# Attention steps in fours: four rounds of scores and maxima, then four value rounds, with twice the buffers between

## The chip, the cores and the metric

One core of a Trainium2 chip runs the whole kernel. The metric is the device time of one launch in microseconds (us). The kernel before ran three times; the profile is one more execution, taken by the hardware profiler.

## The reference

The layer runs over four batches of 2048 tokens with 512 channels. Each batch goes through attention with 16 heads of 32 channels, and then through a mixture of experts (128 experts of which 48 are kept, 8 for each token).

```python
mod = (silu(c) @ wmod).reshape(4, 6, 1, -1)
h = layernorm(x) * (1 + ca) + sa
q, k, v = to_heads(h @ Wqkv.T + bqkv)
att = softmax(where(causal, rope(q) @ rope(k).T * HD ** -0.5, -inf))
x = x + ga * ((att @ v) @ Wo.T + bo)
h = layernorm(x) * (1 + cb) + sb
x = x + gb * mixture_of_experts(h)
```

## The kernel before, in words

**Stages.** A batch passes through three stages: projections of q, k and v with the rotation of q and k (the steps of `front()`, L120); attention, head by head (`stream()`, L160); then the mixture of experts with routing. The change lies in the second.

**Attention.** Scores of a head are computed with keys on the partitions: a *score tile* is 128 keys by the 512 queries of one of four query chunks, 40 tiles of a head (the masked ones narrower). Each is one matmul on PE (L1334; masked tiles have a second, L1337, that adds the mask) into one of three PSUM banks S2, from which ScalarE (ACT) writes the exponential into a probability buffer `Pt` (L1141). The softmax needs each query's maximum beforehand; it comes from 40 *maxima tiles* of the same head with queries on the partitions (L1311, into three PSUM banks S1), reduced by VectorE (DVE) at L1653 or, for masked and some other tiles, L1649. The maxima of a half of the head are turned into a row (L1316 on PE, then DVE) that is moved by SP as a 97th row into the stacked queries `QK` (`max_row`, L736), so that the score matmul subtracts it. The first half of the row serves query chunks 0 and 1, the second half chunks 2 and 3: the first score of chunk 2, which is the first of round 5, waits for it (L1322).

**Rounds.** The score tiles of a chunk go through in *rounds* of two or three tiles (`SHAPES`, L91), 15 rounds of a head: rounds 0 and 1 belong to chunk 0, 2 to 4 to chunk 1, 5 to 8 to chunk 2, and 9 to 14 to chunk 3. For a round GpSimd (POOL) sums its probability tiles into a buffer `Sm` (`plus`, L1006), and then PE runs the *value round*: two or three value matmuls side by side in strips of 32 columns (L1358) and the sum of the probabilities in the fourth strip (L1361, L1362). A value round waits for its sum (L1343). An exponential waits until the value round that last read its `Pt` buffer is done (L1140), a sum until the one that last read its `Sm` buffer is done (L999).

**Order.** `stream()` writes out one list of steps for all engines by hand; each engine runs its own kinds of step in the order of that list. An iteration of its loop (L203) takes two rounds n and n+1: their score tiles alternate with what stands in `beside` for them, then come their sums, then the two value rounds n-2 and n-1, then what stands in `closing`. In `beside` are the maxima of the *next* head, spread from round 2 of a head to round 0 of the following one (`TILES_FROM`, L155), and the steps that make the row. In `closing` are the copies of a finished chunk's output out of PSUM to `od` (ACT, L1128), `LAG` = 3 rounds after the chunk's last round, then the joins, reciprocals and scalings of groups of four heads, and at the end of a batch the first output projections.

**SP's queue.** The loads of heads are issued by SP, in order (L788 to L819). In its loop for head hh SP waits until all scores of head hh-2 have been issued (they read the same half of `QK`), issues the 12 loads of head hh (`stack`, L698), the second half of the row of head hh-1 (L736), the moves of `od` for chunk 3 of head hh-2 and chunk 0 of head hh-1 (`move`, L731, three or four DMAs each, behind the copy), chunk 1, the first half of head hh's row, and the move of chunk 2 of head hh-1. Then come, for one head in four, a load of the next group's values (L719) and, for one in four, a store of a group (L751). Only then does the loop for head hh+1 begin.

**Buffers.** There are 12 `Pt` and 4 `Sm` buffers of 512 columns in float32 (L94), `Pt[:, t % NPT]` and `Sm[:, round % NSM]`.

Of the kernel before, what the change touches and what calls it, by code (L numbers as in the profile page):

```python
# [7 lines left out]
F32 = mybir.dt.float32  # L8
# [4 lines left out]
ACT = mybir.ActivationFunctionType  # L13
AX = mybir.AxisListType

P = 128
NB, T, C, H, HD = 4, 2048, 512, 16, 32
KT = C // P
CH = 512
NCH = T // CH  # L20
# [27 lines left out]
ONE = 1  # L48
# [42 lines left out]
SHAPES = ((2, 2), (3, 2, 3), (3, 3, 3, 3), (3, 3, 3, 3, 2, 2))  # L91
ROUNDS = [(j, tuple(range(sum(shape[:r]), sum(shape[:r + 1])))) for j, shape in enumerate(SHAPES) for r in range(len(shape))]
NR = len(ROUNDS)
NPT, NSM, LAG = 12, 4, 3  # L94
N_JOIN = 2 * NCH - 1
NS1 = NS2 = 3
NCK = NCH * NG
# [9 lines left out]
def tile_at(j, k):  # L107

    return 2 * j * (j + 1) + k
# [50 lines left out]
def stream():  # L160

    closing = [[] for _ in range(NR * H + 12)]
    beside = [[] for _ in range(NR * H)]
    negated = {}
    for i in range(LAST_CHUNK, NTILE):
        beside[(i - LAST_CHUNK) // 4].append(("max", 0, i))
    beside[2].append(("most", 0, 1))
    beside[3] += [("row", 0, 1), ("negated", 0, 1)]
    for hh in range(1, H):
        late = TILES_FROM if hh > 1 else FIRST_TILES_FROM  # L170
        at, span = NR * (hh - 1) + late, NR + 1 - late
        for i in range(NTILE):
            beside[at + i * span // NTILE].append(("max", hh, i))
            if i in (FIRST_HALF - 1, NTILE - 1):
                half, n = int(i >= FIRST_HALF), at + i * span // NTILE
                beside[n + 1].append(("most", hh, half))
                beside[n + 2].insert(0, ("row", hh, half))
                negated[n + 2] = ("negated", hh, half)
    for n, step in negated.items():
        beside[n].insert(2, step)  # L180
    for hh in range(H):
        for j in range(NCH):
            n = NR * hh + LAST_ROUND[j] + LAG
            closing[n].append(("copy", hh, j))
            if hh == H - 1 and j < NCH - 1:
                closing[n + 2] += [("join", NG - 1, j), *(("inverse", NG - 1, j, i) for i in range(TPC))]
                closing[n + 3].append(("scale", NG - 1, j))
            elif hh % GH == GH - 1 and hh < H - 1:
                closing[n + 3].append(("join", hh // GH, j))
                for i in range(TPC):  # L190
                    closing[n + 3 + i // 2].append(("inverse", hh // GH, j, i))
                closing[n + 5].append(("scale", hh // GH, j))
    last = NR * (H - 1)
    for i, t in enumerate(OUT_AT):
        closing[last + t].append(("out", *divmod(i, TPC)))
        if i == TPC - 1:
            closing[last + t].append(("moments",))
    closing[last + NR].append(("normed",))
    closing[NR * (H - 3)].append(("fold",))
    closing[last - 1].append(("widen", 0))  # L200
    closing[last + 5].append(("widen", 1))
    out = []
    for n in range(0, NR * H + 12, 2):  # L203
        if n < NR * H:
            here = [divmod(n, NR), divmod(n + 1, NR)]
            tiles = [("score", hh, r, k) for hh, r in here for k in ROUNDS[r][1]]
            aside = beside[n] + beside[n + 1]
            for i in range(max(len(tiles), len(aside))):
                out += tiles[i:i + 1] + aside[i:i + 1]
            out += [("plus", *of) for of in here]  # L210
        if 2 <= n < NR * H + 2:
            out += [("value", *divmod(n - 2, NR)), ("value", *divmod(n - 1, NR))]
        out += closing[n] + closing[n + 1]
    return out


# [84 lines left out]
def adaln_block(nc, x, wqkv, bqk, bv, wo, bo, cT, wmod, gwT, o2n_col, o2n_row, wgu, wdn, cos, sin, kst, out):  # L301
    with ExitStack() as ctx:
# [74 lines left out]
        stA = place("stA", [P, TPC, 6], F32)  # L377
        mvA = place("mvA", [P, TPC, 2], F32)
        rsA = place("rsA", [P, TPC], F32)
        xin = [place("xin0", [P, TPC, C], F32), xin1]  # L380
        SPARE_AT = at[0]
        vst = [vst0, place("vst1", [P, TPC, NG * P], F32)]


        at[0] = W_AT
        Pt = place("Pt", [P, NPT, CH], F32)
        Sm = place("Sm", [P, NSM, CH], F32)
        o1 = place("o1", [P, T], F32)
        o2 = place("o2", [P, T], F32)
        assert at[0] <= W_END  # L390


        at[0] = OD_AT
# [64 lines left out]
        at[0] = SPARE_AT  # L458
        B1 = place("B1", [P, TPC, 6, P], BF16)
        B2 = place("B2", [P, TPC, 6, 2, P], BF16)  # L460
        stC = place("stC", [P, TPC, 6], F32)
        mvC = place("mvC", [P, TPC, 2], F32)
        rsC = place("rsC", [P, TPC], F32)
# [429 lines left out]
        def _(pool):  # L893
# [21 lines left out]
            for b in batches(pool):  # L915
# [37 lines left out]
                for step in STEPS:  # L953
# [13 lines left out]
                    elif kind == "mul":  # L967

                        _, n, i = step
                        j = n // NG  # L970
                        chunk = NCK * b + n
                        table_of = cs[:, j % 2, i:i + 1].broadcast_to([P, 2, CH])
                        if n % NG == 0 and i == 0:
                            pool.wait_ge(cs_in[j % 2], ONE + 32 * (NCH // 2 * b + j // 2 + 1))
                        if i == 0:

                            pool.wait_ge(f_act, ONE + N_QT * b + taken_by(("proj", n, 1)))
                            if n >= 2:
                                pool.wait_ge(q_lo, ONE + chunk - 1)
                            nc.gpsimd.tensor_tensor(t1[:, n % 2], qraw[:, n % 2], table_of, ALU.mult).then_inc(rope_mul, 1)  # L980
                        else:
                            pool.wait_ge(q_shuf, ONE + chunk + 1)
                            nc.gpsimd.tensor_tensor(qs[:, :, :], qs[:, :, :], table_of, ALU.mult).then_inc(rope_mul, 1)
                    elif kind == "fold":

                        pool.wait_ge(rows_in, ONE + 64 * (b + 1))
                        nc.gpsimd.tensor_tensor(rows[:, 1], rows[:, 0], rows[:, 1], ALU.mult).then_inc(gabo, 1)
                        for k in range(KT):
                            nc.gpsimd.tensor_tensor(wot[:, k], wot[:, k], rows[:, 0], ALU.mult).then_inc(wo_gated, 1)
                    elif kind == "widen":  # L990
                        widen(step[1])
                    elif kind == "plus":

                        _, hh, r = step
                        j, ks = ROUNDS[r]
                        at = NR * hh + r
                        pool.wait_ge(exp_done, ONE + NPT_B * b + NTILE * hh + tile_at(j, ks[-1]) + 1)
                        if at >= NSM:
                            pool.wait_ge(pv_done, ONE + NV * b + at - NSM + 1)  # L999
                        of = [Pt[:, (NTILE * hh + tile_at(j, k)) % NPT] for k in ks]  # L1000
                        for i in range(1, len(ks)):
                            first, _ = extent(j, ks[i])
                            total = Sm[:, at % NSM, first:CH]
                            if i == 2:
                                pool.wait_ge(sum_done, ONE + N_SUM * H * b + N_SUM * hh + SUMS[r] - 1)
                            nc.gpsimd.tensor_tensor(total, of[0][:, first:CH] if i == 1 else total, of[i][:, first:CH], ALU.add).then_inc(sum_done, 1)  # L1006
                    elif kind == "join":
                        join(*step[1:])
                    elif kind == "scale":
                        scale(*step[1:])  # L1010
                    elif kind == "moments":
                        spread_of(0)
# [45 lines left out]
        def _(act):  # L1058
# [18 lines left out]
            for b in batches(act):  # L1077
# [11 lines left out]
                for step in STEPS:  # L1089
# [39 lines left out]
                    elif kind == "score":  # L1129
# [4 lines left out]
                        if t == 0:  # L1134

                            act.wait_ge(w_out, ONE + 16)
                        act.wait_ge(s2_ready, ONE + NPT_B * b + t + 1)
                        if t >= NPT:

                            act.wait_ge(pv_done, ONE + NV * b + NR * ((t - NPT) // NTILE) + ROUND_OF[(t - NPT) % NTILE] + 1)  # L1140
                        nc.scalar.activation(Pt[:, t % NPT, first:CH], S2[t % NS2][:, first:CH], ACT.Exp, scale=SCALE).then_inc(exp_done, 1)  # L1141
                    elif kind == "normed":
                        norm(0)
                meet(act, 2 * b + 2)
# [69 lines left out]
        def _(pe):  # L1214
# [25 lines left out]
            for b in batches(pe):  # L1240
# [18 lines left out]
                for step in STEPS:  # L1259
# [79 lines left out]
                    elif kind == "value":  # L1339
# [12 lines left out]

                            pe.wait_ge(o_free, ONE + NCH * H * b + nn - 1)
                        begins = r == FIRST_ROUND[j]
                        of = [Pt[:, (NTILE * hh + tile_at(j, k)) % NPT] for k in ks]
                        firsts = [extent(j, k)[0] for k in ks]
                        for i, k in enumerate(ks):
                            mm(O[j % 2][i * HD:(i + 1) * HD, firsts[i]:CH], V[:, g % 2, k, h * HD:(h + 1) * HD], of[i][:, firsts[i]:CH],  # L1358
                               start=begins, stop=r == LAST_USE[j, i])
                        if firsts[1] > firsts[0]:  # L1360
                            mm(O[j % 2][3 * HD:P, firsts[0]:firsts[1]], onesv[:, :], of[0][:, firsts[0]:firsts[1]], start=begins, stop=False)  # L1361
                        mm(O[j % 2][3 * HD:P, firsts[1]:CH], onesv[:, :], Sm[:, at % NSM, firsts[1]:CH], start=begins, stop=r == LAST_ROUND[j]).then_inc(pv_done, 1)  # L1362
                    elif kind == "out":
                        rows_out(*step[1:])
                meet(pe, 2 * b + 2)
# [521 lines left out]
```

## Time and profile before

| | |
|---|---|
| three runs | 4260.27, 4262.83, 4269.38 us (median 4262.83) |
| the profiled execution, its span | 4268.8 us |
| PE busy | 3857.2 us, 90% |
| VectorE busy | 2754.6 us, 65% |
| GpSimd busy | 2780.5 us, 65% |
| ScalarE busy | 1806.6 us, 42% |

The span runs from the first to the last instruction of the profiled execution; it is 6 us above the median of the runs and lies between the lowest and the highest. Busy shares are means over all stages. Attention of a batch is some 570 us of it, four times. The wait of an engine is the idle time before an instruction, put down to what released it.

### The profile page before, as it was taken

Reading aid. Unit: us, or ns where it says so; the run is one execution under the profiler, and the core shown is the slowest. Engines: PE = TensorE matmul, PEld = TensorE weight load, DVE = VectorE, ACT = ScalarE, POOL = GpSimd, SP = SyncE. Lnnn points to the kernel's source line nnn. Section 1 sums busy time; section 2 is a strip of 40 time slices with the busy share of each in tenths; the row PEclk is TensorE's granted clock in tenths of the full one; section 3 lists DMA queues with packets and bytes.
Section 4 is the critical chain, followed back from the end, with each engine's and each line's share of the span. In section 5 each row is a group of like instructions: output and inputs, shape, how many; then the busy total and the mean of one; then the engine's idle time right before and its main releaser. Section 6 shows DMA issues by size and latency. Waiting matters only on the chain. (4 is left out here: it accounts for less than half of the span.)

```text
span 4268.8 us, 81098 instructions
## 1 busy us (share of the span) xinstructions
PE 3857.2 (90%) x21344; PEld 2337.8 (55%) x21344; DVE 2754.6 (65%) x5889; ACT 1806.6 (42%) x3526; POOL 2780.5 (65%) x2251
## 2 busy tenths in 40 slices
PE   5989999987999999879899999879899999859998
PEld 2754544456744454457554544457545444547776
DVE  3767677466757767476667776567676774645655
ACT  1345555423355555332355555233455555211111
POOL 3768788824668878716678888427687888215554
PEclk8989999998999999989899999889899999979999
DMA  6543333242533333334433333425333332349997
GB/s 210 180 119 91 91 99 108 79 181 98 178 93 100 86 102 96 120 135 148 139 91 100 99 98 108 155 82 179 115 90 91 99 105 81 102 135 258 258 257 190
DMA packets 305135, 549.12 MB, mean 129 GB/s; under 512 B 59572, under 2 KB 99636, under 8 KB 301492
## 3 DMA queue, kind: packets, MB, share of 16 engines
q1 hardware_dynamic: 283192, 485.62, 37.8%
q0 software_dynamic: 21504, 58.40, 5.8%
q8 instruction: 183, 3.00, 0.3%
q14 instruction: 256, 2.10, 0.2%
HBM read 311.86 MB, written 174.85 MB: 114 GB/s over the span
## 5 line engine op out<-in xcount | busy, mean ns | idle before, releaser
L1141 ACT ACTIVATE Pt<-PS 128x512 f32<-128x512 f32 (+3 forms) x2560 | 1205.9, 542 | 1004.6 <-PE PS L1334 554.9
L1006 POOL TENSOR_TENSOR Sm<-Pt 128x512 f32<-128x512 f32 (+3 forms) x960 | 1029.5, 1078 | 389.6 <-ACT Pt L1141 383.6
L1653 DVE TENSOR_REDUCE part<-PS 128x1 f32<-128x512 f32 x1536 | 1003.5, 685 | 334.6 <-PE PS L1311 329.6
L1311 PE MATMUL PS<-QK 96*128 96x512 f32 (+3 forms) x2560 | 1026.8, 419 | 88.6 <-DVE mT L1668 24.4
L1334 PE MATMUL PS<-QK 97*128 97x512 f32 (+3 forms) x2560 | 991.8, 409 | 38.7 <-DMA QK<-mT 18.5
L1358 PE MATMUL PS<-Pt,V 128*32 128x512 f32 (+3 forms) x5120 | 870.0, 554 | 42.5 <-POOL Sm L1006 42.3
L1362 PE MATMUL PS<-Sm,onesv 128*32 128x512 f32 (+3 forms) x1920 | 818.8, 535 | 0.0
L1649 DVE CUSTOM_DVE_ANT_0 PS<-PS,consts 128x128 f32<-128x128 f32 (+3 forms) x1024 | 503.8, 495 | 415.8 <-PE PS L1311 408.5
L1334 PEld LDWEIGHTS PS<-QK 97*128 97x128 f32 x2560 | 488.0, 193 | 474.7 <-issue 345.7
L1006 POOL TENSOR_TENSOR Sm<-Sm,Pt 128x512 f32<-128x512 f32 (+1 forms) x640 | 713.2, 1114 | 50.2
L1311 PEld LDWEIGHTS PS<-QK 96*128 96x128 f32 x2560 | 496.0, 195 | 299.5 <-DVE part L1653 110.8
L1358 PEld LDWEIGHTS PS<-Pt,V 128*32 128x32 f32 x5120 | 217.1, 111 | 366.0 <-issue 238.1
L1295 PE MATMUL PS<-hTu,W 128*128 128x512 f32 x1024 | 328.3, 402 | 25.3 <-DVEq L644 13.4
L980 POOL TENSOR_TENSOR t<-qraw,cs 128x1024 f32<-128x1024 f32 x64 | 184.4, 2882 | 171.7 <-ACT qraw L1106 162.6
L1042 POOL DMA_INDIRECT out<-z,it x96 | 139.1, 1448 | 208.0 <-DVE z L1831 113.3
L1601 DVE RECIPROCAL den<-den 128x128 f32<-128x128 f32 x256 | 221.2, 914 | 69.4 <-DMA den<-od 67.9
L1461 PEld LDWEIGHTS PS<-XT,Wg 128*96 128x96 f32 x1536 | 250.7, 164 | 26.7 <-issue 26.3
L1461 PE MATMUL PS<-XT,Wg 128*96 128x192 f32 x1536 | 259.2, 327 | 1.3 <-ACT XT L1192 0.7
L1337 PE MATMUL PS<-mtbf,idbf 128*128 128x128 bf16 (+1 forms) x1024 | 239.1, 236 | 0.0
L1295 PEld LDWEIGHTS PS<-hTu,W 128*128 128x128 f32 x1024 | 194.7, 193 | 73.3 <-issue 17.6
L1128 ACT ACTIVATE od<-PS 128x512 f32<-128x512 f32 x256 | 155.6, 608 | 138.3 <-PE PS L1362 138.3
L1106 ACT ACTIVATE qraw<-PS,bqg 128x512 f32<-128x512 f32 x128 | 86.9, 679 | 279.7 <-PE PS L1295 248.9
(169 smaller groups left out, 4962.6 us busy)
## 6 DMA issues: line engine op xcount, KB each, us to landing
QK<-qkd SPq DMA_DIRECT2D x720, 128.0 KB, 3.1
qkd<-st SPq DMA_DIRECT2D x64, 1024.0 KB, 4.5
Wg<-wgu SPq DMA_DIRECT2D x48, 768.0 KB
o<-od SPq DMA_DIRECT2D x448, 64.0 KB, 2.0
W<-wd SPq DMA_DIRECT2D x3, 6144.0 KB, 21.5
Wd<-wdn SPq DMA_DIRECT2D x48, 384.0 KB
xin<-x SPq DMA_DIRECT2D x16, 1024.0 KB, 7.9
vd<-vst SPq DMA_DIRECT2D x16, 1024.0 KB, 6.1
```

The source lines that it names most:

```text
L1006: nc.gpsimd.tensor_tensor(total, of[0][:, first:CH] if i == 1 else total, of[i][:, first:CH], ALU.add).then_inc(sum_done, 1)
L1141: nc.scalar.activation(Pt[:, t % NPT, first:CH], S2[t % NS2][:, first:CH], ACT.Exp, scale=SCALE).then_inc(exp_done, 1)
L1295: last = mm(bank, W[:, w, k, i, g * P:(g + 1) * P], (hTu, hTl)[h][:, j % 2, k], start=(k, w, h) == (0, *TERMS[0]), stop=(k, w, h) == (KT - ...
L1311: mm(s1[:, 0:w], QK[0:3 * HD, hh % 2, 0, qb * P:(qb + 1) * P], QK[0:3 * HD, hh % 2, 1, c * CH:c * CH + w], start=True, stop=True).then_inc ...
L1334: last = mm(S2[t % NS2][:, first:CH], QK[0:3 * HD + 1, hh % 2, 1, k * P:(k + 1) * P], QK[0:3 * HD + 1, hh % 2, 0, j * CH + first:(j + 1) * ...
L1337: last = mm(S2[t % NS2][:, first:first + masked], idbf[:, :], mtbf[:, 2 * P - masked:2 * P], start=False, stop=True)
L1358: mm(O[j % 2][i * HD:(i + 1) * HD, firsts[i]:CH], V[:, g % 2, k, h * HD:(h + 1) * HD], of[i][:, firsts[i]:CH], start=begins, stop=r == LAS ...
L1362: mm(O[j % 2][3 * HD:P, firsts[1]:CH], onesv[:, :], Sm[:, at % NSM, firsts[1]:CH], start=begins, stop=r == LAST_ROUND[j]).then_inc(pv_done, 1)
L1461: last = mm(banks[i][:, q, :], Wg[:, u % HELD, k, o:o + HALF], XT[:, u % 2, k // 2, k % 2, :], start=k == 0, stop=k == KT - 1)
L1601: v.reciprocal(den[:, cols], den[:, cols]).then_inc(den_inv, 1)
L1649: v.tensor_tensor_reduce(out=s1[:, 0:w], in0=s1[:, 0:w], in1=K[:, K_NEG + CH - w:K_NEG + CH], scale=1.0, scalar=-3e38, op0=ALU.add, op1=AL ...
L1653: v.reduce_max(part[:, qb, cc:cc + 1], s1[:, 0:w], AX.X).then_inc(s1_dve, 1)
```

## The change

`BURST` = 4 takes the place of the 2 that stood in the loop of `stream()`: an iteration takes four rounds, whose score tiles alternate with the `beside` of all four, then the four sums, then the four value rounds before these, then the `closing` of four rounds. There are 24 `Pt` and 8 `Sm` buffers, and `LAG` is 4. The second halves of both sets are placed over memory of the projection stage (an input buffer and a buffer of values for `Pt`, the rotation's tables for `Sm`); since that stage's values are stored to HBM from there, ACT waits once a batch for that store before the first exponential into the second half.

```diff
-NPT, NSM, LAG = 12, 4, 3
+BURST = 4
+NPT, NSM, LAG = 24, 8, 4
...
-    for n in range(0, NR * H + 12, 2):
+    for n in range(0, NR * H + 12, BURST):
         if n < NR * H:
-            here = [divmod(n, NR), divmod(n + 1, NR)]
+            here = [divmod(n + i, NR) for i in range(BURST)]
             tiles = [("score", hh, r, k) for hh, r in here for k in ROUNDS[r][1]]
-            aside = beside[n] + beside[n + 1]
+            aside = sum(beside[n:n + BURST], [])
             for i in range(max(len(tiles), len(aside))):
                 out += tiles[i:i + 1] + aside[i:i + 1]
             out += [("plus", *of) for of in here]
-        if 2 <= n < NR * H + 2:
-            out += [("value", *divmod(n - 2, NR)), ("value", *divmod(n - 1, NR))]
-        out += closing[n] + closing[n + 1]
+        if BURST <= n < NR * H + BURST:
+            out += [("value", *divmod(n - BURST + i, NR)) for i in range(BURST)]
+        out += sum(closing[n:n + BURST], [])
     return out
...
-        Pt = place("Pt", [P, NPT, CH], F32)
-        Sm = place("Sm", [P, NSM, CH], F32)
+        Pt0 = place("Pt0", [P, NPT // 2, CH], F32)
+        Sm0 = place("Sm0", [P, NSM // 2, CH], F32)
...
+        at[0] = C_END
+        Sm1 = place("Sm1", [P, NSM // 2, CH], F32)
+        assert at[0] <= W_AT
+        at[0] = XIN_AT
+        Pt1 = place("Pt1", [P, NPT // 2, CH], F32)
+        PT_END = at[0]
+        Pt = [half[:, i] for half in (Pt0, Pt1) for i in range(NPT // 2)]
+        Sm = [half[:, i] for half in (Sm0, Sm1) for i in range(NSM // 2)]
...
                         if t == 0:
 
                             act.wait_ge(w_out, ONE + 16)
+                        if t == NPT // 2:
+
+                            act.wait_ge(v_out[1], ONE + 32 * (NCH // 2) * (b + 1))
```

In the changed kernel's lines the scores are L1350 and L1353, the maxima L1327, the value rounds L1374 to L1378.

PE's list in the kernel before, from value round 8 of head 4 on (32x384, 32x256, 32x128 and the two sums are that round; `V` are the values, `onesv` ones):

```order
L1343 REGISTER_ALU
L1358 MATMUL PS<-Pt,V 32x384
L1358 MATMUL PS<-Pt,V 32x256
L1358 MATMUL PS<-Pt,V 32x128
L1361 MATMUL PS<-Pt,onesv 32x128
L1362 MATMUL PS<-Sm,onesv 32x256
L1343 REGISTER_ALU
L1353 REGISTER_ALU
L1358 MATMUL PS<-Pt,V 32x512 x3
L1362 MATMUL PS<-Sm,onesv 32x512
L1333 REGISTER_ALU
L1334 MATMUL PS<-QK 128x512
```

One value round stands behind it, and then a stretch of scores begins (rounds 12 and 13 of head 4), followed by two value rounds, a second stretch and two more value rounds, before the scores of rounds 1 and 2 of head 5.

PE's list in the changed kernel, from the same value round on:

```order
L1374 MATMUL PS<-Pt_91,V 32x384
L1374 MATMUL PS<-Pt_91,V 32x256
L1374 MATMUL PS<-Pt_91,V 32x128
L1377 MATMUL PS<-Pt_91,onesv 32x128
L1378 MATMUL PS<-Sm_90,onesv 32x256
L1359 REGISTER_ALU
L1369 REGISTER_ALU
L1374 MATMUL PS<-Pt_91,V 32x512 x3
L1378 MATMUL PS<-Sm_90,onesv 32x512
L1359 REGISTER_ALU
L1374 MATMUL PS<-Pt_91,V 32x512 x3
L1378 MATMUL PS<-Sm_90,onesv 32x512
```

The scores of rounds 12 to 14 of head 4 and round 0 of head 5 now stand ahead of this round; three value rounds stand behind it.

PE's list in the changed kernel, behind the last of these value rounds, from the second score tile of round 1 of head 5 to the first maximum of head 6 (`mtbf,idbf` is the mask, `consts,mx` the row of maxima, the ISA row a wait for the head's loads):

```order
L1353 MATMUL PS<-mtbf,idbf 128x128
L1349 REGISTER_ALU
L1350 MATMUL PS<-QK 128x128
L1353 MATMUL PS<-mtbf,idbf 128x128
L1283 REGISTER_ALU
L1331 REGISTER_ALU
L1332 MATMUL PS<-consts,mx 8x128
L1349 REGISTER_ALU
L1350 MATMUL PS<-QK 128x512
L1283 REGISTER_ALU
L1326 ISA
L1327 MATMUL PS<-QK 128x128
```

The same rows stand in the same order ahead of that maximum in the kernel before; there two stretches of scores and four value rounds lie between it and value rounds 8 and 9 of head 4. SP's list has the same order in both kernels.

## Rows read from the trace of the kernel before

**Rows 1.** The page: the span, busy time of the engines, TensorE's granted clock in 40 slices.

```profile
span 4268.8 us, 81098 instructions
...
PE 3857.2 (90%) x21344; PEld 2337.8 (55%) x21344; DVE 2754.6 (65%) x5889; ACT 1806.6 (42%) x3526; POOL 2780.5 (65%) x2251
...
PEclk8989999998999999989899999889899999979999
```

**Rows 2.** Waits of PE: engine, line, releaser, total us, times, longest us.

```profile
PE PS L1358 <- POOL Sm L1006: 42.3, 26, 4.5
...
PE PS L1334 <- DMA QK<-mT: 18.5, 4, 5.2
...
PE PS L1311 <- DMA QK<-qkd: 14.1, 21, 1.5
...
PEld PS L1311 <- DVE part L1653: 110.8, 379, 1.1
```

**Rows 3.** Timeline of PE and ACT, 428 to 442: start, duration, instruction, [idle before <-releaser].

```profile
428.18 0.51 PE L1358 MATMUL PS<-Pt,V 128*32 128x384 f32 x3
...
429.20 0.60 ACT L1128 ACTIVATE od<-PS 128x512 f32<-128x512 f32 x1 [0.66 <-PE PS L1362]
...
435.26 0.22 PE L1334 MATMUL PS<-QK 97*128 97x128 f32 x1
...
441.43 0.33 PE L1311 MATMUL PS<-QK 96*128 96x128 f32 x1 [1.32 <-DMA QK<-qkd]
```

**Rows 4.** Timeline of SP's issues, 432 to 445.

```profile
432.68 0.66 SPq L719 DMA_DIRECT2D V<-vd  x1
435.79 7.88 SPq L698 DMA_DIRECT2D QK<-qkd  x12
443.86 0.73 SPq L736 DMA_DIRECT2D QK<-mT  x1
```

**Rows 5.** Timeline of PE around two value rounds, 612 to 615.

```profile
612.00 0.40 PE L1334 MATMUL PS<-QK 97*128 97x512 f32 x1
612.23 0.28 PE L1311 MATMUL PS<-QK 96*128 96x256 f32 x1
612.45 0.63 PE L1358 MATMUL PS<-Pt,V 128*32 128x512 f32 x3
...
613.76 0.61 PE L1358 MATMUL PS<-Pt,V 128*32 128x512 f32 x3
...
614.30 0.50 PE L1334 MATMUL PS<-QK 97*128 97x512 f32 x1
614.64 0.23 PE L1337 MATMUL PS<-mtbf,idbf 128*128 128x128 bf16 x1
```

**Rows 6.** Timeline of SP and PE at the start of a batch's attention, 250 to 262.

```profile
250.33 7.79 SPq L698 DMA_DIRECT2D QK<-qkd  x12
258.33 0.76 SPq L736 DMA_DIRECT2D QK<-mT  x1
...
254.81 0.44 PE L1311 MATMUL PS<-QK 96*128 96x128 f32 x1 [0.54 <-DMA QK<-qkd]
...
261.14 0.79 PE L1334 MATMUL PS<-QK 97*128 97x512 f32 x1 [4.45 <-DMA QK<-mT]
```

**Rows 7.** Windows: from:to us, busy (x count) PE PEld DVE ACT POOL, PEclk, DMA, GB/s.

```profile
382.70:389.00 6.30, 5.07 (x34) 2.66 (x30) 6.30 (x13) 3.20 (x6) 6.14 (x7) 1.00 0.14 34
...
676.00:683.60 7.60, 6.34 (x34) 3.23 (x30) 7.44 (x14) 3.26 (x6) 6.92 (x8) 0.78 0.13 32
...
441.30:446.00 4.70, 4.48 (x28) 2.50 (x29) 2.40 (x10) 2.84 (x6) 2.53 (x2) 1.00 0.67 194
```

**Rows 8.** Timeline of PE at a batch's tail, 832.

```profile
832.52 0.78 PE L1358 MATMUL PS<-Pt,V 128*32 128x512 f32 x3 [2.72 <-POOL Sm L1006]
```

**Rows 9.** Timeline of DVE, 381 and 611: a group's reciprocals, maxima.

```profile
381.88 3.38 DVE L1601 RECIPROCAL den<-den 128x128 f32<-128x128 f32 x4
...
611.26 1.89 DVE L1653 TENSOR_REDUCE part<-PS 128x1 f32<-128x512 f32 x3
```

More of the change, by code:

```diff
@@ L379, in adaln_block @@
         rsA = place("rsA", [P, TPC], F32)
+        XIN_AT = at[0]
         xin = [place("xin0", [P, TPC, C], F32), xin1]
@@ L460, in adaln_block @@
         B2 = place("B2", [P, TPC, 6, 2, P], BF16)
+        assert at[0] >= PT_END
         stC = place("stC", [P, TPC, 6], F32)
@@ L999, in _ @@
                             pool.wait_ge(pv_done, ONE + NV * b + at - NSM + 1)
-                        of = [Pt[:, (NTILE * hh + tile_at(j, k)) % NPT] for k in ks]
+                        of = [Pt[(NTILE * hh + tile_at(j, k)) % NPT] for k in ks]
                         for i in range(1, len(ks)):
                             first, _ = extent(j, ks[i])
-                            total = Sm[:, at % NSM, first:CH]
+                            total = Sm[at % NSM][:, first:CH]
                             if i == 2:
@@ L1140, in _ @@
                             act.wait_ge(pv_done, ONE + NV * b + NR * ((t - NPT) // NTILE) + ROUND_OF[(t - NPT) % NTILE] + 1)
-                        nc.scalar.activation(Pt[:, t % NPT, first:CH], S2[t % NS2][:, first:CH], ACT.Exp, scale=SCALE).then_inc(exp_done, 1)
+                        nc.scalar.activation(Pt[t % NPT][:, first:CH], S2[t % NS2][:, first:CH], ACT.Exp, scale=SCALE).then_inc(exp_done, 1)
                     elif kind == "normed":
@@ L1354, in _ @@
                         begins = r == FIRST_ROUND[j]
-                        of = [Pt[:, (NTILE * hh + tile_at(j, k)) % NPT] for k in ks]
+                        of = [Pt[(NTILE * hh + tile_at(j, k)) % NPT] for k in ks]
                         firsts = [extent(j, k)[0] for k in ks]
@@ L1361, in _ @@
                             mm(O[j % 2][3 * HD:P, firsts[0]:firsts[1]], onesv[:, :], of[0][:, firsts[0]:firsts[1]], start=begins, stop=False)
-                        mm(O[j % 2][3 * HD:P, firsts[1]:CH], onesv[:, :], Sm[:, at % NSM, firsts[1]:CH], start=begins, stop=r == LAST_ROUND[j]).then_inc(pv_done, 1)
+                        mm(O[j % 2][3 * HD:P, firsts[1]:CH], onesv[:, :], Sm[at % NSM][:, firsts[1]:CH], start=begins, stop=r == LAST_ROUND[j]).then_inc(pv_done, 1)
                     elif kind == "out":
```

## The prediction

> **What bounds the kernel now.** I read the page's head first: TensorE is busy 90% of the span, VectorE and GpSimd 65% each, and the clock line sits at 8 or 9 tenths throughout [rows 1]. So PE's own list of work sets the time, and the next question is what makes PE wait. The waits of PE show that attention hardly waits: maxima on VectorE's emptying no more than 1.1 us at a time, maxima on the head's loads (QK<-qkd) 14.1 us in 21 waits, scores on the row of maxima (QK<-mT) 18.5 us in 4, value rounds on GpSimd's sums 42.3 us in 26 [rows 2]. The last three are small *because* the work that they wait for is started early enough. The change moves where that work starts, so I then followed one head through the timelines.
>
> Call H the head whose scores run. During H come the maxima of head H+1, and for those its q and k have to be loaded. SP's queue is in order (L788 to L819): the copy of chunk 2 of head H-1 goes out (L731, four DMAs), then, every fourth head, V (L719) or a group's store, then the 12 loads of head H+1 (L698), then the second half of H's row of maxima (L736). The move cannot start before ACT has copied the chunk out of PSUM (L1128), and that waits for value round 8 of head H-1. Thus *value round 8 of head H-1 on PE, copy, move, loads, first maximum of head H+1* is one chain, and *... loads, row, score of round 5 of head H* another.
>
> For H = 5: round 8 of head 4 starts at 428.18, the copy runs 429.20 to 429.80, the move follows, V is issued at 432.68 for 0.66 [rows 3, 4]; there SP waits until 435.79, since the loads may not overwrite head 4 before its last score at 435.26 [rows 3, 4]. The 12 loads take 7.88, the row is issued at 443.86, and the first maximum runs at 441.43, 5.6 after the loads began and after a wait of 1.32 [rows 3, 4]. So 11.6 us lay between the copy's end and the first maximum, and PE still came early by 1.3.
>
> **The cost of a late chain.** Prices: round 8's start to the copy's end 1.62, of it some 0.8 after PE is free of the round (a round is 0.93: two from 612.45 to 614.30 [rows 5]); copy's end to SP's next issue behind the move 2.9 (429.80 to 432.68), 3.5 with a group's store (0.6, an estimate from the other issues), 3.8 with V [rows 3, 4]; loads to first maximum 5.6 behind a V load, 4.5 without (250.33 to 254.81 at a batch's start) [rows 4, 6]; loads to the row's issue 7.7 to 8.1; the row's issue to the score that needs it 2.8 (258.33 to 261.14) [rows 6].
>
> In the changed kernel four score rounds stand together, then four value rounds, and the fours run over heads of 15 rounds, so four cases come in turn. A matmul of a score stretch is 0.24 [rows 5].
> H = 1, 5, 9, 13: round 8 is the first of its four (the first piece of PE's list above). Behind it PE has three value rounds (2.7) and four matmuls (1.0), then the first maximum: 3.7 us of work against 0.8 + 3.8 + 5.6 = 10.2. PE waits 6.5.
> H = 4, 8, 12: two value rounds and some 12 matmuls, 1.85 + 2.9 = 4.7, against 0.8 + 3.5 + 4.5 = 8.8: 4.1.
> H = 3, 7, 11: one value round and some 18 matmuls, 0.9 + 4.4 = 5.3, against 0.8 + 2.9 + 4.5 = 8.2: 2.9.
> H = 2, 6, 10, 14: round 8 is the last of its four; a whole score stretch follows and four value rounds, so the first maximum is in time (8.4 against 8.2), but the score of round 5 comes after 4.3 + 3.6 + 3.0 = 10.9, against 0.8 + 2.9 + 7.7 + 2.8 = 14.2: 3.3.
> A batch has 4 x 6.3 (one of the four lacks V) + 3 x 4.1 + 3 x 2.9 + 4 x 3.3 = 59 us, four batches **+237** in 56 waits. In the kernel before the same distances hold one more score stretch, and that covered the chain.
>
> **The clock.** After a wait PE can run at the lower of its two levels: a stretch of the same 34 matmuls takes 6.30 at a granted clock of 1.00 (2.4 GHz) and 7.60 at a mean of 0.78, which is 0.50 (1.2 GHz) in 44% of it [rows 7]: 1.3 us. Not every wait is followed by that: behind the wait of 1.32 at 441.43 the clock is 1.00 for 4.7 us [rows 3, 7]. Bounds: 0, and 56 x 1.3 = 73. The waits here are mostly longer than those, so I take **+45**.
>
> **Ends.** At a batch's start two value rounds now run after, not inside, the 4.45 us wait for the row [rows 6]: 2 x 0.93, +1.8. At the tail the output projection is placed behind more of GpSimd's work, and value rounds already wait 2.72 for their sum there [rows 8]: I take +2.7. Times four: **+18**. Four such places are few; 0 and 36 are the bounds.
>
> **Gains.** A round trip between value and score shapes costs PE 0.30: 0.22 behind a 256-column maximum worth 0.12, the last value row 0.54 where those before it took 0.44 each (612.45 to 613.76, three), the first score 0.34 for 0.24 [rows 5]. 480 round trips become 240: -72 at most. Part comes back: VectorE takes 0.63 for a maximum of 512 columns (1.89 for three), PE issues one every 0.48, and three PSUM banks hold no more than three of them [rows 5, 9]. In the kernel before the two value rounds let VectorE catch up; in fours it falls behind for longer, then catches up for longer. I take **-45** (0 to -72). More buffers loosen the value rounds' wait on sums, 42.3 us in all [rows 2], and the value rounds in fours cover more of the four reciprocals' 3.38, which keep VectorE from the maxima [rows 9]: **-20** (0 to -42). The added wait on ACT for a store of V before the thirteenth exponential comes once a batch and behind SP's own wait for it (L787): nothing, as scores wait for the row of maxima there until 261.14 [rows 6]. The buffers' new places cost nothing: they are the same operations on other addresses, and the inputs that lay there are used up.
>
> **Sum.** 237 + 45 + 18 - 45 - 20 = +235. The profiled execution has a span of 4268.8, 6 above the median of 4262.83 and within the three runs; against the median 4262.8 + 235 = **4498**. What a measurement of this kernel can tell from no change is about 0.2%, 8.5 us. The likeliest case's own range: with each of the 56 chains 1.5 shorter -84, with the clock at 73, no gain from fewer round trips and the ends at 36 +91: 4400 to 4590.
>
> **Rivals.** (A) *Faster: the chain is not late.* The place is SP's loads (L698). If they began earlier than I count, PE would keep only the gains and the ends: 4262.8 - 65 + 18 = 4216 (4190 to 4250). It decides at each head: the time from the copy's end to the first maximum has to be no more than the 3 to 4.5 us of work that PE has left. For it speaks that the 12 loads are not held up by anything else there; against it that their issue alone is 0.65 apiece, one behind the other (7.88 for 12), and that the wait of 1.32 at 441.43 shows no slack today [rows 3, 4]. Chance 0.12.
> (B) *Half the waiting.* The waits fall together with VectorE's arrears: where VectorE sets the stretch anyway, a wait for the loads of 3 to 6 us takes the place of waits for emptying rather than adding to them. Then 118 + 22 + 18 - 45 - 20 = +93: 4356. For it: ten full maxima are 6.3 us of VectorE, the 20 matmuls with them 4.8 of PE [rows 5, 9]. Against: those arrears are at most three banks, 1.9 us [rows 9]. Chance 0.10.
> (C) *The lower clock stays.* After each wait the whole of the next score stretch and its value rounds run low, two stretches of 1.3 more: 56 x 2.6 = 148 in place of 45, 4601. For it: a stretch partly at 0.50 is in the trace [rows 7]; against it: the other stretch of the same work ran at 1.00, so did the one behind the wait at 441.43, and the clock line stands at 8 and 9 tenths [rows 1, 7]. Chance 0.10. The Trainium skill (TensorE: Matmul & The Clock Gate, "HAM oscillation — how this bites in real kernels") says that a kernel whose short runs of matmuls each follow a wait on a DMA starts every one of them at the low clock; by that rule the time would be (C)'s; the trace of before doesn't bear it out at 441.43, where the clock is 1.00 behind the wait, but that wait is short.
> (D) *No change*, gains and waits within 8.5 of each other: 4263, chance 0.02. PE's list shows that the fours are really there, so the change does what it says.
>
> **How the numbers follow.** The likeliest case has 0.66, (A) 0.12, (B) 0.10, (C) 0.10, (D) 0.02. The range 4320 to 4610 holds the likeliest, (B) and (C), 0.86 less their tails. Faster by over 0.2%: 0.12; within: 0.02; slower: 0.86.
>
> **What would show it.** In the waits of PE, maxima on QK<-qkd should grow from 14.1 us to some 150 to 190, and scores on QK<-mT from 18.5 to 60 or 70. SP's loads should begin within 4 us of a copy's end, with no wait for the last score between. The head after a V load should wait longest, near 6.5. Wrong I would be if QK<-qkd stays near 14 us (then A), or if it grows and PE's waits on VectorE fall by as much (B), or if the clock line drops by a tenth in all of attention (C).

## The result, and the profile after

Four runs took 4651.39 to 4658.54 us, median 4654.51; the kernel before, in the same comparison, 4262.15. The ratio is 1.0915, with a 95% interval of 1.090 to 1.093: slower by 392 us. The forecast was slower by 235, 4498, with a range from 4320 to 4610. The direction and the place were right, the size was not.

The page of the changed kernel (the span, the engines, the granted clock in 40 slices), which answers to [rows 1]:

```profile
span 4653.8 us, 81110 instructions
...
PE 3999.0 (86%) x21344; PEld 2506.1 (54%) x21344; DVE 2753.6 (59%) x5889; ACT 1824.4 (39%) x3526; POOL 2784.6 (60%) x2251
...
PEclk8978888888988988888888888889888898879999
```

The span grew by 385. PE has the same 21344 matmuls, but is busy 142 us longer, while VectorE's and GpSimd's busy time stands still (ScalarE's grew by 18); and the clock line has lost about a tenth through most of attention. That is one part. The waits of PE (engine, line, releaser, total us, times, longest), which answer to [rows 2], show another:

```profile
PE PS L1327 <- DMA QK<-qkd: 221.0, 47, 9.0
PE PS L1350 <- DMA QK<-mT: 58.4, 22, 4.8
PE PS L1271 <- issue: 33.1, 3, 11.1
...
PE PS L1271 <- POOL ot L959: 9.4, 1, 9.4
```

Waiting for a head's loads and for the row of maxima came to 279.4 us in place of 32.6, +247; the prediction had +237, without the batches' starts. The value rounds' wait for sums (42.3 before) is gone from the list. The output projections at a batch's end (L1271), which did not appear there, wait 42.5.

The same head as in [rows 3, 4], now from 464 to 478 us. First ACT, then SP's issues, then PE:

```profile
464.77 0.60 ACT L1141 ACTIVATE od<-PS 128x512 f32<-128x512 f32 x1 [1.62 <-PE PS L1378]
```

```profile
465.46 0.56 SPq L744 DMA_DIRECT2D ot<-od  x1
...
469.03 0.66 SPq L732 DMA_DIRECT2D V<-vd  x1
470.02 7.83 SPq L711 DMA_DIRECT2D QK<-qkd  x12
478.19 0.72 SPq L749 DMA_DIRECT2D QK<-mT  x1
```

```profile
463.76 0.51 PE L1374 MATMUL PS<-Pt,V 128*32 128x384 f32 x3
...
467.63 0.48 PE L1350 MATMUL PS<-QK 97*128 97x512 f32 x1
476.94 0.47 PE L1327 MATMUL PS<-QK 96*128 96x128 f32 x1 [8.83 <-DMA QK<-qkd]
```

Value round 8 starts at 463.76, the copy ends at 465.37, SP goes straight through move, V and loads without a wait between, and PE, done with its other value rounds and four matmuls by 468.1, stands still until 476.94. The chain is the one that was described; two prices in it were a little low (copy's end to loads 4.65 where I had 3.8, loads to first maximum 6.9 where I had 5.6; both are with a V load in front).

What the clock does around such a wait (from:to, length, busy time (x count) of PE, PEld, DVE, ACT, POOL, then granted clock, DMA share, GB/s):

```profile
305.00:312.90 7.90, 7.90 (x31) 4.66 (x33) 4.95 (x16) 3.42 (x7) 4.96 (x5) 0.51 0.30 80
350.70:357.30 6.60, 6.60 (x34) 3.64 (x33) 2.52 (x7) 0.69 (x2) 2.56 (x2) 0.52 0.04 10
473.50:476.90 3.40, 0.00 (x0) 0.00 (x0) 0.00 (x0) 0.00 (x0) 0.00 (x0) 0.50 1.12 258
476.90:487.00 10.10, 10.06 (x42) 6.42 (x45) 4.96 (x16) 3.42 (x7) 4.97 (x5) 0.51 0.39 88
487.20:492.90 5.70, 5.58 (x29) 3.18 (x22) 3.57 (x10) 4.74 (x10) 2.34 (x2) 1.00 0.21 49
```

The clock falls while PE waits (473.50 to 476.90, no matmul at all), stays at the lower level, 1.2 GHz, for 10 us of work behind the wait, and is back at 2.4 GHz from 487.2 on. In the first batch each of the 14 waits for a head's loads or its row, 2.3 to 8.8 us long, is followed by such a stretch, 6 to 11 us of work; the wait of 2.4 us at 346.3 has its own at 350.7. In the kernel before the waits of 1.2 to 1.3 us in attention mostly had none [rows 7]: in the first batch one of seven did. Over the whole span the lower clock stood for 438 us before and for 1008 us now, summed over its stretches in the traces; 2 x (1 - mean granted clock) x span, with means of 0.949 and 0.892, gives the same within 3 us.

### The profile page after: what moved, and what is told of

It is laid out like the page before. It is cut to its first block and busy times, and to the rows that moved or that the text cites. A ratio compares the mean times of both kernels' runs of the same rounds, so it can differ in the third digit from the quotient of the medians.

```text
span 4653.8 us, 81110 instructions
## 1 busy us (share of the span) xinstructions
PE 3999.0 (86%) x21344; PEld 2506.1 (54%) x21344; DVE 2753.6 (59%) x5889; ACT 1824.4 (39%) x3526; POOL 2784.6 (60%) x2251
## 5 line engine op out<-in xcount | busy, mean ns | idle before, releaser
L1019 POOL TENSOR_TENSOR Sm<-Pt 128x512 f32<-128x512 f32 (+3 forms) x900 | 957.8, 1072 | 687.3 <-ACT Pt L1157 681.3
L1327 PE MATMUL PS<-QK 96*128 96x512 f32 (+3 forms) x2560 | 1107.3, 447 | 263.2 <-DMA QK<-qkd 221.0
L1350 PE MATMUL PS<-QK 97*128 97x512 f32 (+3 forms) x2560 | 1028.5, 419 | 78.5 <-DMA QK<-mT 58.4
L1374 PE MATMUL PS<-Pt,V 128*32 128x512 f32 (+3 forms) x5120 | 900.0, 596 | 0.0
L1378 PE MATMUL PS<-Sm,onesv 128*32 128x512 f32 (+3 forms) x1920 | 856.7, 573 | 0.0
L1327 PEld LDWEIGHTS PS<-QK 96*128 96x128 f32 x2560 | 538.9, 212 | 496.9 <-DVE part L1669 138.6
L1350 PEld LDWEIGHTS PS<-QK 97*128 97x128 f32 x2560 | 517.7, 205 | 349.1 <-issue 212.0
L1374 PEld LDWEIGHTS PS<-Pt,V 128*32 128x32 f32 x5120 | 312.6, 119 | 401.8 <-issue 267.4
L1353 PE MATMUL PS<-mtbf,idbf 128*128 128x128 bf16 (+1 forms) x1024 | 248.7, 244 | 0.0
L1271 PE MATMUL PS<-wot,otc 128*128 128x512 f32 x384 | 196.0, 651 | 42.6 <-issue 33.1
```

The source lines that it names most:

```text
L1327: mm(s1[:, 0:w], QK[0:3 * HD, hh % 2, 0, qb * P:(qb + 1) * P], QK[0:3 * HD, hh % 2, 1, c * CH:c * CH + w], start=True, stop=True).then_inc ...
L1350: last = mm(S2[t % NS2][:, first:CH], QK[0:3 * HD + 1, hh % 2, 1, k * P:(k + 1) * P], QK[0:3 * HD + 1, hh % 2, 0, j * CH + first:(j + 1) * ...
L1353: last = mm(S2[t % NS2][:, first:first + masked], idbf[:, :], mtbf[:, 2 * P - masked:2 * P], start=False, stop=True)
L1378: mm(O[j % 2][3 * HD:P, firsts[1]:CH], onesv[:, :], Sm[at % NSM][:, firsts[1]:CH], start=begins, stop=r == LAST_ROUND[j]).then_inc(pv_done, 1)
```

## The experiments

Two theories. **Theory 1:** the loads of the next head are queued on SP behind the copy of value round 8, which fours make late; PE waits for them, and works at the lower clock after each wait. **Theory 2:** fours are slow in themselves, since VectorE falls behind in a longer stretch of scores and maxima, or since the buffers' places cost something.

### Loads ahead of the moves

Only SP's order changes. (In the chunks below `behind_loads` holds the move of chunk 2, the V load and the group's store that stood at the end of the loop.)

```diff
                     max_row(hh - 1, 1)
                     if hh >= 2:
+                        behind_loads(hh - 1)
                         move(hh - 2, NCH - 1)
...
-                    move(hh - 1, 2)
-                    if h == 1 and g + 1 < NG:
-                        load_values(g + 1)
-                    if h == 0 and g < NG:
-                        store_group(g - 1, range(1))
+                behind_loads(H)
```

> The changed kernel with one thing moved on SP: the move of chunk 2 of the head before, and the V load or group's store behind it, come behind the next head's 12 loads and the row of maxima, so that the loads start as soon as the scores allow, not behind value round 8. Theory 1 (the loads are late behind value round 8, and each wait is followed by a stretch at the lower clock): PE's waits on QK<-qkd fall from 221 us to under 60, the low-clock time from 1008 us to 400 to 600, and the time to 4200 to 4320. Theory 2 (fours are slow in themselves: VectorE falls behind in the longer stretch): the time stays above 4500.

Measured: 4377.91 (4368.68 to 4379.35), 1.0253 of before, interval 1.0236 to 1.027. Its waits of PE:

```profile
PE PS L1356 <- DMA QK<-mT: 37.7, 23, 4.9
...
PE PS L1333 <- DMA QK<-qkd: 32.2, 16, 6.2
...
PE PS L1277 <- issue: 29.6, 3, 10.9
...
PE PS L1277 <- POOL ot L965: 10.9, 1, 10.9
```

Another order in SP's queue, eleven added lines, takes 277 of the 392 us away. The wait for loads went from 221.0 to 32.2 and the low-clock time from 1008 to 645. Theory 2 is out as the main cause. The time missed theory 1's range by 58 at the top, though, and the low-clock time by 45: 115 us stay that the late loads do not explain. A part of them are waits that were small under the late loads: PE's maxima now wait for VectorE, 37.2 us where they waited 5.5 in the changed kernel; twelve of these waits, three in a batch, are 2.3 to 3.3 us long. In the first batch each of its three stands behind a group's reciprocals and has a stretch at the lower clock behind it (from 417.9, 568.1 and 721.7):

```profile
PE PS L1333 <- DVE part L1675: 37.2, 29, 3.3
```

```profile
412.19 3.39 DVE L1623 RECIPROCAL den<-den 128x128 f32<-128x128 f32 x4 [2.09 <-DMA den<-od]
...
416.18 0.44 PE L1333 MATMUL PS<-QK 96*128 96x384 f32 x1 [2.37 <-DVE part L1675]
```

### Throwaway matmuls in the wait

The wait stays, but PE works in it: 12, then 24 matmuls of 96x512 ahead of a head's first maximum, into the bank that it overwrites.

```diff
+                        if i == 0 and hh >= 2:
+                            for _ in range(12):
+                                mm(s1[:, 0:CH], QK[0:3 * HD, (hh + 1) % 2, 0, 0:P], QK[0:3 * HD, (hh + 1) % 2, 1, 0:CH], start=True, stop=True)
                         if qb % TPC == 0 and c == 0:
 
                             pe.wait_ge(qk_in
```

> The changed kernel with 12 throwaway matmuls of 96x512 ahead of a head's first maximum (56 times), into the bank that the maximum then overwrites. They fill some 2.9 us of the wait for the loads and change no other wait. If the lower clock comes from PE's idling, the low-clock time falls by a third or more from 1008 us and the time from 4654 to 4480 to 4600. If the clock falls for another reason, or costs nothing there, the time is 4640 to 4700: the 12 matmuls only take the place of waiting, and cost where there was none.

> The changed kernel with 24 in place of 12 throwaway matmuls ahead of a head's first maximum, some 5.7 us, more than most of its waits. If PE's idling is what brings the lower clock, PE's low-clock time goes back to 440 to 520 us, and the time is 4480 to 4570, though the fill alone takes some 320 us of PE and the waits that it replaces were 279. If the clock does not answer to the fill: above 4620.

Measured: 4565.06 (4559.54 to 4570.37) with 12, 4627.11 (4624.04 to 4629.99) with 24, against 4654.51 without. The group of the 12 in the first (busy us, mean ns), and then what the waits came to in it:

```profile
L1326 PE MATMUL PS<-QK 96*128 96x512 f32 x672 | 162.9, 391 | 0.0
```

```profile
PE PS L1330 <- DMA QK<-qkd: 114.9, 35, 5.9
...
PE PS L1353 <- DMA QK<-mT: 22.5, 17, 4.7
```

More work, less time. The sum by spans: 12 add 162.9 of matmuls and take 142.0 of waiting away (279.4 to 137.4), so PE's list should have grown by 21; the span fell by 89.2 (to 4564.6). The difference, 110, came with 345 us less of the lower clock (1008 to 663). With 24: 315.3 added, 199.6 of waiting gone, span 26.3 less; the difference, 142, came with 448 us less (1008 to 560). Both times a microsecond at the lower clock costs 0.32. The 24 missed their range (4480 to 4570) mainly because they took 199.6 us of waiting away and not the 279 that I had counted on; the clock, which came back to 560 and not to 440 to 520, is the smaller part (40 us of it by 0.32 are 13). That PE's idling brings the lower clock is shown. Its price in the changed kernel is an estimate: 570 us more of it by 0.32, some 180 us. PE's busy time without the throwaway matmuls fell by 114 for 345 us and by 155 for 448, and with the loads first by 98 for 363 (3999.0 to 3901.5): 0.27 to 0.35 each, so 150 to 200 us.

### Buffers alone, and threes

```diff
-BURST = 4
-NPT, NSM, LAG = 24, 8, 4
+BURST = 2
+NPT, NSM, LAG = 24, 8, 3
```

> The changed kernel with twos again (BURST 2, LAG 3) and the 24 probability and 8 sum buffers kept. Theory 1: the order is that of the kernel before, so 4245 to 4275. If the buffers' places or the added wait on ACT cost something: above 4290.

Measured: 4263.92, ratio 0.9995, interval 0.9985 to 1.0005. In twos, places, added wait and twice the buffers cost nothing and bring nothing. With BURST = 3 in the same place:

> The changed kernel with threes (BURST 3, LAG 3): five iterations a head, so value round 8 is always the last of its three, and a score stretch and three value rounds lie between it and the next head's first maximum. Theory 1: PE's waits on QK<-qkd under 60 us, time 4190 to 4300. Theory 2 (longer stretches are slow in themselves): half of the way to fours, 4400 to 4500.

Measured: 4279.43, ratio 1.0026, interval 1.0013 to 1.0038. The range of theory 1 holds, the waits for loads are 30.4 and those for the row 17.8, and the mean clock is 0.949 as before. But threes have 160 round trips fewer than twos and gained nothing. Summed over the timeline, the 320 value stretches take 821 us where 480 took 866. But 42 of these 45 us are the wait for GpSimd's sums, which fell from 42.3 to 0.5; some 3 are left for the round trips. The score stretches, each from its first score or maximum to the next value round, take 1634 in place of 1581: there the gain is lost. In them PE itself waits for the row's maxima, 1.8 us before and in threes:

```profile
PE PS L1332 <- DVE mx L1675: 55.7, 64, 1.0
```

And PE's weight loads for maxima wait longer on VectorE's reductions, 179 us before and 227 in threes; the largest row, 110.8 before [rows 2], is in threes:

```profile
PEld PS L1327 <- DVE part L1669: 173.6, 537, 1.1
```

### A maximum leads each pair

To see whether VectorE's pace took the gain: the alternation turned round, so that VectorE starts one matmul earlier.

```diff
-                out += tiles[i:i + 1] + aside[i:i + 1]
+                out += aside[i:i + 1] + tiles[i:i + 1]
```

> Threes with the alternation turned round: a maximum leads each pair, then a score. VectorE begins a stretch one matmul (0.24 us) earlier, nothing else changes. If VectorE's pace sets the end of a stretch of nine maxima (why the 160 round trips fewer of threes brought nothing), the time falls from 4279 by 30 to 80 us to 4200 to 4250 and PE's weight loads wait less for VectorE (173.6 us in threes). If something else gave the gain back, 4265 to 4290.

> Twos (the order of the kernel before, larger buffers) with a maximum leading each pair. If VectorE's pace sets only the longer stretches, little changes: 4240 to 4270; as much gain as in threes would say that the order of the pair helps by something other than a stretch's length.

> Fours with the loads ahead of the moves (the run of 4378) and a maximum leading each pair. If the longest stretches are set by VectorE, 20 to 80 us less than 4378: 4300 to 4360. If what is left there is the lower clock and the output projection's wait, 4360 to 4395.

Measured: threes 4216.98 (ratio 0.9888, interval 0.9873 to 0.9903), 62 less than threes; twos 4226.20 (0.9916, 0.9901 to 0.9931), 38 less than twos; fours with the loads first 4330.74, 47 less. The order of the pair is worth something at every length, so the forecast that twos would hardly gain (4240 to 4270) was wrong. It is worth more in threes than in twos, as VectorE's pace would have it, but in fours, with the longest stretches, less than in threes. The weight loads' wait on VectorE did not fall in threes (181.9, from 173.6), which I had expected, and in twos nearly all of the gain stands in PE's busy time (3859.7 to 3817.5) and not in a wait. How the earlier start saves the time is not shown.

Two maxima ahead of the pairs, in threes:

> Threes with two maxima leading the stretch in place of one, then pairs. VectorE never idles between the first maxima, and the last steps of a stretch are scores. If VectorE's pace still sets the stretch: 10 to 40 us less than 4217, 4180 to 4207. If one leading maximum already gave what was there: 4210 to 4230.

Measured: 4254.19, 37 *more* than with one. Neither forecast holds, and I have no explanation that a run supports. One row that grew with it is the weight loads' wait on VectorE's reduction of masked and some other tiles, from 38.8 to 72.6; whether that is the cause is left open.

### The row's step two maxima later

```diff
-                beside[n + 2].insert(0, ("row", hh, half))
                 negated[n + 2] = ("negated", hh, half)
     for n, step in negated.items():
-        beside[n].insert(2, step)
+        beside[n].insert(2, ("row", *step[1:]))
+        beside[n].insert(4, step)
```

> Threes, a maximum leading each pair, and the step that turns a half's maxima into a row placed two maxima later. In threes this step stands in the same stretch as the last maxima of its half and waits for them on VectorE (47.0 us of PE's waits). If that wait is PE's loss, it falls below 15 us and the time to 4175 to 4210; if it only moves to other maxima, as VectorE's pace would have it, 4205 to 4225.

> Twos, a maximum leading each pair, and the row's step two maxima later, as in the run of 4195 with threes. In twos the row stands an iteration behind its half's last maxima, so it has little to wait for: 4210 to 4235. Threes then keep a lead of 15 to 40 us, which is what fewer round trips are worth once VectorE's pace is out of the way; if twos come to 4200 or less, the round trips are worth nothing.

Measured: threes 4195.04 (4186.75 to 4196.52), ratio 0.9835, interval 0.9822 to 0.9849; twos 4218.14, 0.9898, 0.9881 to 0.9914. The first of these rows is the row's wait in threes with a maximum leading, the second in the run with the later row:

```profile
PE PS L1332 <- DVE mx L1675: 47.0, 64, 1.3
```

```profile
PE PS L1332 <- DVE mx L1675: 7.7, 8, 1.3
```

Threes gained 22 us by it, of 39 us of waiting gone. Threes now lead twos by 23. That is not shown to be the price of the round trips: in the twos value rounds wait 56.9 us for GpSimd's sums, in threes 10.5, a difference larger than the lead.

```profile
PE PS L1374 <- POOL Sm L1019: 56.9, 51, 4.6
```

The threes with the later row are the fastest of all, 70 us below the kernel before in its comparison (4264.96).

### The output projections an iteration later

The last piece of fours: with the loads and the maxima first, the projections at a batch's end are placed four rounds later.

```diff
-OUT_AT = (10, 10, 11, 12, 13, 14, 15, 16)
+OUT_AT = (14, 14, 15, 16, 17, 18, 19, 20)
```

> Fours with the loads ahead of the moves and a maximum leading each pair (the run of 4331), the first output projections at a batch's end placed four rounds later, an iteration of fours. If their wait for GpSimd (32.1 + 11.3 us, 4 times) is PE's loss, it falls below 10 us and the time to 4285 to 4310. If the wait only moves to other steps of the tail: 4320 to 4340.

Measured: 4294.93 (4290.19 to 4300.57), 36 less. Before the edit PE's first row below stood at 32.1, and the second at 11.3; after it:

```profile
PE PS L1277 <- issue: 4.9, 3, 1.6
...
PE PS L1277 <- POOL ot L965: 1.7, 1, 1.7
```

So the wait was PE's loss almost in full. The timeline of the changed kernel, first GpSimd, then PE, shows what it waits for:

```profile
917.38 4.55 POOL L942 TENSOR_TENSOR xc<-xc,rows 128x2048 f32<-128x2048 f32 x1
...
929.59 1.26 POOL L1019 TENSOR_TENSOR Sm<-Sm,Pt 128x512 f32<-128x512 f32 x1
930.80 1.26 POOL L949 TENSOR_TENSOR ot<-ot,o 128x512 f32<-128x512 f32 x1
932.23 1.26 POOL L959 TENSOR_TENSOR ot<-ot,den 128x512 f32<-128x512 f32 x1 [0.17 <-POOL ot L949]
```

```profile
933.59 1.19 PE L1271 MATMUL PS<-wot,otc 128*128 128x512 f32 x1 [11.13 <-issue]
```

The scaled output that the projection needs stands on GpSimd behind a widening and eight sums, since an iteration puts four rounds' sums ahead of its joins and scalings. It ends at 933.49; PE goes on at 933.59.

## Why the prediction was right or wrong

The span's +385, by the terms of the sum:

| term | predicted | measured | from |
|---|---|---|---|
| waits for loads and row inside attention | +237 | +227 | waits of PE, 11.4 to 238.8 |
| the lower clock | +45 | some +180 | 570 us more of it, 0.32 each by the two fills |
| ends | +18 | +62 | the same waits at a batch's start, 21.2 to 40.6, and the output projection's wait, 42.5 |
| gains | -65 | some -84 | what remains |

**The chain was right**, place and size. The four cases gave 6.5, 3.3, 2.9 and 4.1 us. In the first batch the waits are 8.3, 2.4, 2.4, 4.5, 8.8, 2.7, 2.5, 4.4, 8.3, 2.3, 2.7, 3.7, 4.9 and 2.8: the longest where a V load lies in the chain, the third case and the last near their numbers, and 61 us in all where I had 59; over four batches the 56 waits come to 236.7. That this meets 237 so closely is partly luck: the heads behind a V load waited some 2 us longer than their sum, the second and third case 0.2 to 1.1 less. That it was SP's order and not the fours themselves is shown by the run with the loads first.

**The step that failed is the clock**, the term of +45. I wrote "After a wait PE can run at the lower of its two levels", and priced it with one stretch, 7.60 us with the clock low in 44% of it, or 3.3 us, at a cost of 1.3, for some 35 of the 56 waits, because the trace of before had a wait of 1.32 with nothing behind it. But the waits that I forecast were two to five times as long as those that I had looked at. All 14 of the first batch brought the lower clock, for 6 to 11 us of work, and over the span it stood 570 us longer, 10 for each of the 56 waits in place of 3.3 for some of them. The price of a microsecond (1.3 by 3.3, 0.39) was near what the fills give; how often and how long the clock stays low was wrong, and cost some 180 us where I had 45. The rival (C), the lower clock through two stretches after each wait, was the better sum (148 for this term), and I gave it 0.10. For (C) the Trainium skill (TensorE: Matmul & The Clock Gate, "HAM oscillation — how this bites in real kernels") says that runs of matmuls which each follow a wait on a DMA start at the low clock; the windows above agree, and two fills show that idling is its cause. I had set that rule aside on the strength of one short wait.

**The ends** were right in their mechanism, GpSimd's queue at the tail, and too small: I took 2.7 a batch from a wait of 2.72 [rows 8], without counting the sums that four rounds put ahead of the scaling. They are 10.6. At a batch's start the two value rounds no longer run ahead of the first maximum that needs new loads, and it waits 5.74 where it waited 0.54 [rows 6]; with the row's wait that is 4.9 a start, where I had 1.8:

```profile
253.71 0.45 PE L1327 MATMUL PS<-QK 96*128 96x128 f32 x1 [5.74 <-DMA QK<-qkd]
```

**The gains** are what the account leaves, and only that. The value rounds' wait for sums went entirely (-42.3, where I took -20 for it and the reciprocals). PE's waits on VectorE nearly cancel: for emptied banks 29.0 to 11.4 (the row's matmul included), for turned maxima (`mT`) 24.4 to 12.4, for the row's maxima 1.8 to 28.3. That leaves some 40 us, which hang on the clock's price. The round trips' 0.30 each is not confirmed as a gain: in threes 160 fewer of them brought some 3 us in the value stretches. (B), waits that take the place of VectorE's arrears, is there but small: the maxima's wait for emptied banks fell from 29.0 to 8.1 under the late loads and stood at 39.8 with the loads first.

**(A)**, that the chain would not be late, is refuted by SP's rows; (D) by the result. Three slips in the prediction's sums change none of this: 56 x 2.6 in (C) is 146 and not 148, the lower end of the likeliest case's own range is 4414 (4498 - 84) and not 4400, and by its own prices the head without a V load waits 4.5, so that the first case's mean is 6.0 and not 6.3, 5 us in all.

What stays open: why a leading maximum saves time and two save less than one, and what would bring fours with all three remedies (4294.93) up to the kernel before, 0.8% ahead of them. There PE still waits 79.4 us for loads and row (32.6 before) and 59.0 for emptied banks (29.0 before), and the lower clock stands for 570 us, at a mean of 0.934, against 438.

## What to carry to other kernels

When steps are grouped more coarsely on one engine, look for in-order queues in which a load stands behind a result of the moved steps: here another order of a DMA queue, eleven added lines, was worth 277 us, and no engine's busy share showed it. Price a wait on PE by what follows it too, the matmuls at the lower clock, from rows with waits of the length that you forecast, not shorter ones. And fewer switches between kinds of work need not pay by themselves: threes were no faster than twos until the maxima led, and what they gained in the value rounds was a wait for sums, not the switch.

## What the runs showed that was not expected

Adding 672 matmuls that compute nothing made the kernel 89 us faster (4654.51 to 4565.06), since they kept PE at the higher clock for longer (low-clock time 1008 to 663 us). And turning round the order of each pair of score and maximum, one line, was worth 38 us in twos and 62 in threes, about what the whole change was to gain (65).
